# Prologue of a clustering and 1x1 convolution kernel: weights and centroids loaded in a transposed layout, sums of unit 0 in bf16 parts, one add of squares on VectorE

## The reference

```python
xn = x / jnp.maximum(jnp.linalg.norm(x, axis=1, keepdims=True), EPS)
cn = centroids / jnp.maximum(jnp.linalg.norm(centroids, axis=1, keepdims=True), EPS)
sim = jnp.einsum('bchw,nc->bnhw', xn, cn)
idx = jnp.argmax(sim, axis=1)
onehot = jax.nn.one_hot(idx, N, dtype=x.dtype)
sum_x = jnp.einsum('bhwn,bchw->bnc', onehot, x)
count = jnp.sum(onehot, axis=(1, 2))
centroids_local = sum_x / jnp.maximum(count, 1.0)[..., None]
gathered = centroids_local[jnp.arange(B)[:, None, None], idx]
delta = jnp.transpose(gathered, (0, 3, 1, 2)) - x
alpha = jnp.exp(-jnp.mean(delta * delta, axis=1, keepdims=True))
y = x + alpha * delta
out = jnp.einsum('oc,bchw->bohw', W, y) + b[None, :, None, None]
return jax.nn.relu(out)
```

## Time and profile before

| | us |
|---|---|
| median of 3 runs | 409.74 (409.43 to 411.05) |
| profiled execution, own time | 410.88 |
| its span in the profile | 409.1 |
| TensorE busy | 403.9 (99%) |
| VectorE busy | 338.9 (83%) |
| GpSimd busy | 262.1 (64%) |
| ScalarE busy | 260.7 (64%) |

### The profile page before, as it was taken

How to read it: one execution, slowest core, us unless ns; L and a number is a source line. 1 busy time by engine, 2 the same in 40 slices (tenths; PEclk the granted TensorE clock), 3 DMA queues, 4 the chain that set the end, 5 groups by cost and what they waited for, 6 DMA issues and landing times.

```text
span 409.1 us, 5812 instructions
## 1 busy us (share of the span) xinstructions
PE 403.9 (99%) x2088; PEld 288.2 (70%) x2088; DVE 338.9 (83%) x415; ACT 260.7 (64%) x362; POOL 262.1 (64%) x117
## 2 busy tenths in 40 slices
PE   8999999999999999999999999999999999999997
PEld 5746376775867677775867758776777758777886
DVE  2439999888899879999799898998799897898730
ACT  6566783767665684665865576656846658676641
POOL 2003773984599676994789946996769947433420
PEclk9999999999999999999999999999999999999999
DMA  7992493988499395967979575994957240222213
GB/s 256 380 248 51 88 244 84 297 252 180 172 246 266 113 281 140 272 162 183 265 198 229 191 163 188 254 256 118 276 139 226 104 129 13 103 103 104 103 68 138
DMA packets 77918, 74.51 MB, mean 182 GB/s; under 512 B 13723, under 2 KB 52891, under 8 KB 77891
## 3 DMA queue, kind: packets, MB, share of 16 engines
q1 hardware_dynamic: 77890, 74.15, 64.7%
HBM read 46.22 MB, written 25.17 MB: 174 GB/s over the span
## 4 chain that ended last, share of the span: by engine, by line
PE 95%; POOL 1%; DMA 1%; ACT 1%; issue 0%; DVE 0%; SPq 0%; ACTq 0%
PE main L1023 21%; PE main L1024 21%; PE main L1025 21%; PE fa L915 11%; PE sump L960 8%; PE gat L1000 5%; PE fa L924 1%; PE al L1006 1%; DMA x<-x 1%; PE main L1084 1%; PE main L1037 1%; PE al L1011 1%; POOL o L382 1%; POOL o L385 1%; PE gat L1037 1%; PE main L1055 0%
## 5 line engine op out<-in xcount | busy, mean ns | idle before, releaser
L1023 PE MATMUL main<-yh,wh 128*128 128x512 f32 (+1 forms) x376 | 152.8, 406 | 0.0
L1024 PE MATMUL main<-yl,wh 128*128 128x512 f32 (+1 forms) x376 | 146.3, 389 | 0.0
L1025 PE MATMUL main<-yh,wl 128*128 128x512 f32 (+1 forms) x376 | 146.1, 389 | 0.0
L360 POOL TENSOR_TENSOR z<-z,x 128x1024 f32<-128x1024 f32 x41 | 97.4, 2395 | 60.5 <-DVE z L519 60.5
L367 POOL TENSOR_TENSOR yl<-z,yh 128x1024 fp32r<-128x1024 f32 x43 | 103.7, 2429 | 13.8 <-ACT yh L693 13.7
L701 ACT ACTIVATE o<-main,bcol 128x512 f32<-128x512 f32 x96 | 65.1, 680 | 46.8 <-PE main L1025 45.9
L1023 PEld LDWEIGHTS main<-yh,wh 128*128 128x128 f32 x376 | 70.7, 188 | 21.4 <-issue 4.6
L1025 PEld LDWEIGHTS main<-yh,wl 128*128 128x128 f32 x376 | 70.6, 188 | 14.9
L1024 PEld LDWEIGHTS main<-yl,wh 128*128 128x128 f32 x376 | 70.7, 188 | 13.8
L374 POOL TENSOR_TENSOR xr<-xt 128x2048 f32<-128x2048 f32 x11 | 51.5, 4684 | 19.1 <-DVE xt L411 19.1
L483 DVE TENSOR_TENSOR z<-gat,x 128x1024 f32<-128x1024 f32 x46 | 55.8, 1213 | 6.1 <-PE gat L1000 6.1
(11 more groups left out here) (139 smaller groups left out, 402.6 us busy)
## 6 DMA issues: line engine op xcount, KB each, us to landing
out<-o SPq DMA_DIRECT2D x23, 1024.0 KB, 7.2
x<-x SPq DMA_DIRECT2D x21, 1024.0 KB, 6.6
xs<-x SPq DMA_DIRECT2D x76, 256.0 KB, 5.5
x<-x SPq DMA_DIRECT2D x12, 256.0 KB, 5.4
o<-w SPq DMA_DIRECT2D x1, 1024.0 KB, 8.4
out<-o SPq DMA_DIRECT2D x3, 256.0 KB, 2.0
out<-o SPq DMA_DIRECT2D x2, 128.0 KB, 1.7
oht<-oh SPq DMA_TRANSPOSE x7, 3.7
```

Of the source, the lines that this page charges most:

```text
L360: pool.tensor_tensor(z, z, X[g // PARTS % 2][:, pair(h), span(g)], ALU.add).then_inc(y_pool, 1)
L1023: t_.matmul(tile, WH[:, k, rows], YH[g % 2][:, k, cols], start=(k == 0), stop=False)
L1024: t_.matmul(tile, WH[:, k, rows], YL[g % 2][:, k, cols], start=False, stop=False)
L1025: last = t_.matmul(tile, WL[:, k, rows], YH[g % 2][:, k, cols], start=False, stop=(k == KC - 1))
```

## The change

The transposed centroids are a second input, `cent_t`, made on the host, and go straight to `c_t` by the first transfer of SyncE; the rows are still loaded, for their norms, now from ScalarE's queue. The weights are transposed on the host, so `high_weights` and `low_weights` read them in `OUT[0]`, and TensorE's 16 weight transposes and its four of the centroids are gone. In `c_t` the chunks stand 40 columns apart, and a matmul reads 64.

Unit 0's sums are made from bf16 parts: GpSimd makes `first_rest(0)`, VectorE `second_rest(0)`, and unit 0 is the last of its batch in `sum_order`. TensorE does the first chunk of unit 0 (similarities and transposes) ahead of the other chunks, and the other transposes of its second half behind the similarities of unit 2. Units 4 and 5 are turned in four steps of two tiles instead of five steps. VectorE's `transpose_half(3, ...)` stand earlier.

The add of unit 1's two sums of squares moves from GpSimd to VectorE, behind `y_half(0, 1)`, and the product with ones of unit 1 stands behind the first eight matmuls of `high_passes` instead of before them. On ScalarE `exp(1)` stands behind `copy_sums(1)`.

```diff
@@ the split and the order of sums
 def split(g):
-    return g > 2 * PARTS and g % PARTS < SPLIT
+    return g == 0 or g > 2 * PARTS and g % PARTS < SPLIT
-    return (0, 1, 2) if b == 0 else (1, 2, 0) if b == 1 else (2, 0, 1)
+    return (1, 2, 0) if b < 2 else (2, 0, 1)
@@ SyncE
-            sp.dma_start(craw[0:N, :], cent).then_inc(c_in, 16)
+            sp.dma_start(cT[:, 0:KC * N], cent_t).then_inc(cT_in, 16)
@@ GpSimd
             def first_rest(g):
-                pool.wait_ge(tr_done, by_vector(g))
+                if g == 0:
+                    pool.wait_ge(xe_dve, 1)
+                    pool.wait_ge(xe_act, 1)
+                else:
+                    pool.wait_ge(tr_done, by_vector(g))
...
+                if g > 0:
+                    return
                 pool.wait_ge(two_done, 2 * g + 2)
                 first_two, last_two = squares(g, 0)[:, 0, :], squares(g, 1)[:, 0, :]
                 pool.tensor_tensor(first_two, first_two, last_two, ALU.add).then_inc(four_done, 1)
+            first_rest(0)
             add_chunks(0)
             add_chunks(1)
@@ VectorE
+            def add_halves_of_squares(g):
+                dve.wait_ge(two_done, 2 * g + 2)
+                first_two, last_two = squares(g, 0)[:, 0, :], squares(g, 1)[:, 0, :]
+                v_.tensor_tensor(first_two, first_two, last_two, ALU.add).then_inc(four_done, 1)
...
             first_best(0)
-            low_weights(0)
-            low_weights(1)
+            second_rest(0)
+            for k in range(KC):
+                low_weights(k)
             low_clusters(0)
             counts(0)
-            low_weights(2)
             rest_of_mean(0)
             parts_of_mean(0)
-            low_weights(3)
+            transpose_half(3, 0)
             delta(0, 0)
             delta(0, 1)
-            transpose_half(3, 0)
+            transpose_half(3, 1)
             best_sims(1)
             first_best(1)
             delta(1, 0)
             delta(1, 1)
-            transpose_half(3, 1)
             scale(0, 0)
             y_half(0, 0)
             scale(0, 1)
             y_half(0, 1)
+            add_halves_of_squares(1)
             fold_clusters(1)
+            low_clusters(1)
             scale(1, 0)
-            low_clusters(1)
             scale(1, 1)
@@ ScalarE
             high_half(0, 0)
             move_sums(1)
-            exp(1)
             high_half(0, 1)
             copy_sums(1)
+            exp(1)
             count_onehot(1)
@@ TensorE
-            similarities(0)
-            transpose_x(0, 0)
+            similarities(0, range(0, 1))
+            transpose_x(0, 0, range(0, 1))
+            transpose_x(0, 1, range(0, 1))
+            similarities(0, range(1, KC))
+            transpose_x(0, 0, range(1, KC))
             similarities(1)
-            transpose_x(0, 1)
             similarities(2)
+            transpose_x(0, 1, range(1, KC))
+            transpose_sims(0)
             transpose_x(1, 0)
-            transpose_sims(0)
             transpose_x(1, 1)
             transpose_x(2, 0)
             transpose_x(2, 1)
-            transpose_weights(0)
-            transpose_weights(1)
...
-            transpose_weights(2)
-            add_halves(0)
-            transpose_weights(3)
             pe.wait_ge(x_in[1][1], 16)
             turn(0)
+            add_halves(0)
+            turn(1)
             similarities(3)
             similarities(4)
             gather(0, 0)
             gather(0, 1)
             similarities(5)
-            turn(1)
+            turn(2, (0,))
             transpose_sims(1)
-            turn(2)
+            turn(2, (1,))
             turn(3)
-            turn(4)
             gather(1, 0)
+            gather(1, 1)
             sum_squares_direct(0)
-            gather(1, 1)
...
             gather(2, 0)
-            sum_squares_direct(1)
             pe.wait_ge(z_done, 4)
+            pe.wait_ge(wl_done, KC)
             pe.wait_ge(hi_done, 1)
             high_passes(range(0, 2))
+            sum_squares_direct(1)
             pe.wait_ge(hi_done, 2)
             high_passes(range(2, KC))
             add_halves(1)
```

More of the change, by code:

```diff
@@ L790, in _ @@
             keep_transposed(2, 1)
-            high_weights(0)
-            high_weights(1)
             copy_onehot(0)
+            for k in range(KC):
+                high_weights(k)
             copy_sums(0)
             evacuate_onehot()
-            high_weights(2)
             scale_means(0)
             high_means(0)
-            high_weights(3)
             keep_turned(0)
@@ L893, in _, with similarities @@
             t_ = nc.tensor
-            def similarities(g):
+            def similarities(g, ks=range(KC)):
                 b, u = divmod(g, PARTS)
@@ L904, in similarities @@
                 rows = X[b % 2]
-                for k in range(KC):
+                for k in ks:
                     if b == 0:
@@ L1027, in convolve, with transpose_x @@
                     last.then_inc(main_done, 1)
-            def transpose_x(u, half):
+            def transpose_x(u, half, ks=range(KC)):
                 if (u, half) == (1, 0):
@@ L1035, in transpose_x, with turn @@
                     at = u * UNIT + (HALF * half + t) * P
-                    for k in range(KC):
+                    for k in ks:
                         last = t_.transpose((gat, main)[half][:, t, k * P:(k + 1) * P], X[0][:, k, at:at + P],
                                             ident[:, :])
-                last.then_inc(xp_done, 1)
-            def turn(step):
+                if ks[-1] == KC - 1:
+                    last.then_inc(xp_done, 1)
+            def turn(step, now=(0, 1)):
                 g, tiles = TURNS[step]
-                if step == 0:
-                    pe.wait_ge(wl_done, 1)
-                elif step < 3:
-                    pe.wait_ge(z_done, step)
-                else:
-                    pe.wait_ge(xe_act, KEPT + step - 1)
-                for i, t in enumerate(tiles):
-                    at = g % PARTS * UNIT + t * P
+                if step < 2:
+                    pe.wait_ge(xe_act, KEPT - 1 + step)
+                else:
+                    pe.wait_ge(z_done, step - 1)
+                for i in now:
+                    at = g % PARTS * UNIT + tiles[i] * P
                     for k in range(KC):
@@ L1056, in turn @@
                                             ident[:, :])
-                last.then_inc(xp_done, 1)
+                if now[-1] == 1:
+                    last.then_inc(xp_done, 1)
             def keep_busy(times):
```

75 lines of the change are left out of this document (29 added, 46 removed).

## The result

The changed kernel takes **412.03 us** (median of 8 runs, 411.60 to 412.96). The kernel before, timed beside it, takes 410.69 (8 runs, 409.43 to 411.16). The ratio is 1.0044, 95% interval 1.0032 to 1.0056: slower by about 1.8 us. The forecast was 410.8, 1.1 above 409.74, with "within 0.5%" as the likeliest class and slower by over 0.5% at 0.15. The time lies inside the range of 408.0 to 412.2, and the ratio lies close to 0.5%; but the change does make the kernel slower by more than the forecast said.

A forecast was written before the change was run, and what follows sets the result against it. TensorE (busy 403.9 of 409.1 us) and, from 40 to 60 us, VectorE were taken as full. A 1.1 gain by t0 and 2.2 lost after it put the mark 1.1 later: 409.74 becomes 410.8, range 408.0 to 412.2.

The forecast's parts named there:

- The block (main case): VectorE's new add behind y (0,1) waits for GpSimd's first yl, some 2.9 instead of 0.69; 410.8 us, chance 0.52.
- Rival A: The add on VectorE isn't blocked and takes 0.69, with GpSimd's yl stretched to 4; 408.5 us, chance 0.26.
- The mark: First weight load of convolution (0,2), taken for the whole prologue; forecast at 56.45 instead of 55.35, 1.1 slower.
- From t0 to unit 2's first difference: VectorE's stretch, 12.66 before; 12.6 if nothing blocks, but with the block from 39.5 to 54.45.
- t0: Start of unit 1's first difference on VectorE; forecast at 39.5 instead of 40.65, 1.1 earlier.
- The start to the sums: Without the first eight weight transposes, batch 0's sums start at 19.7 instead of 20.70, 1.0 earlier.
- From the sums to t0: Unit 3's blocks land by 30.7, before VectorE's moved transposition needs them, so the early gain of 1.1 lasts.
- Passed on one for one: Behind 60 us the same matmuls follow, so what the first 55 us gain or lose reaches the end unchanged.
- The base: The kernel before's median of 409.74, from which the forecast of 410.8 was counted.
- B: Rival: TensorE alone decides, so all its savings show, 2.9 in all; 406.8 us, chance 0.05.
- D: Rival: the early gain (1.1) and the later loss (2.2) cancel, no net effect; 409.7 us, chance 0.05.
- C: Rival: the path returns to GpSimd's second add of squares, y (0,0) loses another 1.3; 412.1 us, chance 0.12.

The follow-up runs named there:

- e4: The kernel before with only the add of unit 1's halves moved to VectorE and the order that goes with it; 413.21 us, ratio 1.0072 to before.
- e5: The changed kernel with both VectorE transpositions of unit 3's blocks put back where they stood before; 412.41 us, ratio 1.0044 to before.
- e7: The changed kernel's start with the old order behind it, and two products with ones instead of the halves' add; 409.96 us, ratio 0.9986 to before.
- e10: The changed kernel's start, the old order from the second argmax on, the add on GpSimd and the padded centroid tile; 409.44 us, ratio 0.9979 to before.
- e15: e10 repeated unchanged; 409.36 us, ratio 0.9966 to before.
- e3: The changed kernel with VectorE's add ahead of y_half(0, 1) instead of behind it; 412.62 us, ratio 1.0070 to before.

## Why the prediction was wrong, point by point

- **The block (main case).** Right, as a mechanism and in its place: an add of 2.86 where "some 2.9" was forecast, at the end of GpSimd's first `yl`, which had waited. Rival A (0.69) is refuted by e4 as well. The mark, forecast at 56.45, came at 55.91 and 56.91 in two executions.
- **From t0 to unit 2's first difference.** Predicted 14.95, measured 14.43 (39.44 to 53.87), before 12.66. A term mis-sized by 0.5. Half of it is `y_half(0, 0)`, which was to stand behind GpSimd's first add of squares and end at t0 + 5.0. It kept its 1.24 from 42.95, t0 + 3.5, and ended at t0 + 4.75; GpSimd's second add, issued at 43.07, stood behind it (2.26). The other half came in small steps from there to t0 + 14.43. To the mark 16.95 was forecast and 16.47 measured, so the block with the order around it costs 16.47 - 14.70 = 1.77, and not 2.25.
- **The start to the sums.** Right in kind: 19.7 predicted, 19.39 and 19.35 measured, and a gain of some 0.9 in the mean where 1.0 was forecast. The parts of unit 0 are hidden, as forecast.
- **From the sums to t0: the step that failed.** "Its blocks, by their issue and landing, are there at 30.7." They were there at 31.31, 32.32, 31.81, 32.06, 31.27 and 31.02. Little else held VectorE: where the blocks don't matter (e5, e7, e10, e15) 19.4 lie between the sums and t0, and in the changed kernel 20.05 and 21.10. The prediction took 1.1 of gain at t0. It was 1.2 in one execution and 0.2 in the other (40.65 to 39.44 and 40.45), and 0.7 in the mean over the eight profiled executions of this order (39.71, beside 40.37 in four with before's start). Over all executions it was less still, by the estimate: t0 at 40.1 before, and at 39.95 in the 14 of the changed kernel. A landing time of SyncE's queue was used as one number, and a wait that the kernel before had 4 us of slack against was given none. Beside that, the 40.65 from which the gain was counted came from an execution that was late itself.
- **"Passed on one for one" behind the mark.** Wrong by a small amount that every profiled execution repeats: 0.31, from addresses. The edit that packs the centroids was read as an edit of the prologue only.
- **The sum.** In the profiled executions: at t0 -0.7, from t0 to the mark +1.77, behind it +0.31, in all +1.4. The ratios of 1.0044 and 1.0055 give +1.8 (interval 1.3 to 2.3) and +2.3 (1.7 to 2.8). With -0.1 at t0, from the estimate over all executions, the sum is +2.0, so what is missing from +1.4 is the start's scatter. (The estimate is made from the times themselves; what it adds is that only the start differs from one execution to the next.) The forecast had -1.15, +2.25 and 0. Its right sign, and a time inside its range, are in part luck: it gave the start 1.0 too much, the block 0.5 too much, and 0.3 was missing.
- **The base.** 409.74 was the median of three runs; in the four later series of runs before had medians of 410.09 to 410.66, and 410.69 beside the changed kernel. That puts 0.4 to 0.9 of the difference between 410.8 and 412.03 in the base, not in the change.
- **Rivals.** B and D fall with the mark. C's price (412.1) is near the time, but its place is not where it went: `y_half(0, 0)` lost nothing.

The Trainium skill, "SBUF — State Buffer", section "Who interferes with whom", has the block as a rule: a VectorE instruction with two SBUF inputs and a GpSimd instruction that reads SBUF exclude each other. The rows shown agree: in e3 GpSimd's instruction keeps its length (2.38), and VectorE's add stands for nearly the whole of it (2.92 instead of 0.69); in the changed kernel and in e4 the add takes 2.86.

## What to carry to other kernels

A two-input SBUF instruction on VectorE is to be priced with the GpSimd instruction that is released beside it, and not at its own length: an add priced at 0.69 took 2.85 to 2.92 in all nine profiled executions that had it. When work moves to the front of a stage, ask for each load it reads how much slack it had, and take the latest landing that could be, not one row's. A gain early in a pipeline can be lost to what was moved with it: nearly the same start with the old order behind it gained 0.9 to 1.4 us, and with the new one lost 1.8. And before a gain is counted from one profiled execution, ask how late that execution was: here the kernel before scattered by 1.9 us at t0, more than the whole effect at the start.

## What the hardware showed

- Moving seven small constant tiles by 288 bytes per partition made 0.31 us of difference over 24 units, the same in every profiled execution (351.36 to 351.39 in nine executions, 351.01 to 351.07 in eight), with the same matmuls at a granted clock of 0.999 to 1.000. Which tile it is, and why, is not shown.
- Of two instructions that came to a free path 0.01 us apart, the earlier one went first, whichever engine it was on: in e3 GpSimd's at 45.32 ahead of VectorE's at 45.33, in the changed kernel VectorE's at 45.35, which kept its 1.23, ahead of GpSimd's at 45.36.
- The first 20 us vary by about 1.2 us between executions (sums at 19.54 to 20.75 with one and the same start), and everything behind is shifted by that. The time from t0 to the mark, and from there to the end, repeats within 0.06 us where the order and the addresses are the same, so two single executions are best compared there. What makes the start vary is not shown.
